# A Mamba-style mixer between two feed-forward layers: its scan in chunks of 64 positions where it went in chunks of 128

## The reference

```python
x_c, A_c, B_c, C_c = (chunk(x), chunk(Adt), chunk(Bmat), chunk(Cmat))      # CHUNK = 64
A_cum = jnp.cumsum(A_c, axis=-1)
L = jnp.exp(_segsum(A_c))                                                 # decay inside a chunk
G = jnp.einsum('bclhn,bcshn->bclsh', C_c, B_c)
Y_diag = jnp.einsum('bclsh,bcshp->bclhp', G * L, x_c)
decay_states = jnp.exp(A_cum[..., -1:] - A_cum)
states = jnp.einsum('bclhn,bclhp->bchpn', B_decay, x_c)                   # new state of each chunk
new_states = jnp.einsum('bhzj,bjhpn->bzhpn', decay_chunk, states)         # carried over the chunks
Y_off = jnp.einsum('bclhn,bchpn->bclhp', C_c, states) * state_decay_out[..., None]
y = Y_diag + Y_off + D * x
```

## Time and profile before

| | us |
|---|---|
| median of three runs | 1905.34 |
| the profiled execution | 1909.31 |
| its span, first to last instruction | 1907.5 |
| TensorE busy | 1723.2 (90%) |
| VectorE busy | 1076.9 (56%) |
| ScalarE busy | 654.0 (34%) |
| POOL busy | 436.8 (23%) |
| `decay` on TensorE, 512 matmuls | 114.4 |
| `ydiag`, 2048 records | 69.2 |
| `times_g` on VectorE, 184 | 183.8 |
| decay exponentials, 256 | 149.0 |

### The profile page before, as it was taken

How to read it: one execution, slowest core, us unless ns; L and a number is a source line. 1 busy time by engine, 2 the same in 40 slices (tenths; PEclk the granted TensorE clock), 3 DMA queues, 4 the chain that set the end, 5 groups by cost and what they waited for, 6 DMA issues and landing times.

```text
span 1907.5 us, 24623 instructions
## 1 busy us (share of the span) xinstructions
PE 1723.2 (90%) x9444; PEld 1374.8 (72%) x9444; DVE 1076.9 (56%) x1830; ACT 654.0 (34%) x1002; POOL 436.8 (23%) x310
## 2 busy tenths in 40 slices
PE   2369999976999997999998999998899998998998
PEld 0157777754888776888776788776788886777787
DVE  8953334355566755567665466766375754443233
ACT  1222222215443355433345333445334434112111
POOL 7632443010123231212232122322122323000000
PEclk7779999987999998999998899999899999999999
DMA  5373564534344443344434344444445444555564
GB/s 230 156 296 101 209 206 176 183 101 141 119 156 156 135 147 123 113 159 157 148 124 135 118 154 141 160 130 138 130 157 159 141 131 146 152 187 166 187 188 143
DMA packets 248784, 295.66 MB, mean 155 GB/s; under 512 B 11105, under 2 KB 209889, under 8 KB 238689
## 3 DMA queue, kind: packets, MB, share of 16 engines
q1 hardware_dynamic: 248672, 294.14, 46.4%
HBM read 247.97 MB, written 46.14 MB: 154 GB/s over the span
## 4 chain that ended last, share of the span: by engine, by line
PE 61%; DVE 11%; ACT 3%; issue 2%; DVEq 0%; ACTq 0%
PE bank L931 26%; PE bank L971 11%; PE bank L899 11%; PE bank L1009 3%; PE bank L1034 3%; PE bank L987 3%; DVE m_cv L1517 1%; DVE res L1503 1%; PE bank L1048 1%; PE bank L1064 1%; DVE xn L1491 1%; DVE m_L L1544 1%; DVE m_hb L1497 1%; DVE m_sta L1557 1%; PE bank L1022 1%
## 5 line engine op out<-in xcount | busy, mean ns | idle before, releaser
L931 PE MATMUL bank<-m_fxT,m_wj 128*128 128x512 f32 x2304 | 553.1, 393 | 12.7 <-DVE m_fxT L1484 4.6
L931 PEld LDWEIGHTS bank<-m_fxT,m_wj 128*128 128x128 f32 x2304 | 429.2, 189 | 105.3 <-issue 10.0
L971 PE MATMUL bank<-m_wd,m_hb 128*128 128x512 f32 x1152 | 295.2, 399 | 10.4 <-DVE res L1503 5.4
L899 PE MATMUL bank<-m_xT,m_wi 128*128 128x512 f32 x912 | 241.7, 417 | 13.8 <-DVE m_cv L1517 11.4
L971 PEld LDWEIGHTS bank<-m_wd,m_hb 128*128 128x128 f32 x1152 | 209.8, 190 | 54.6 <-issue 7.5
L1827 POOL TENSOR_TENSOR m_L<-m_L,m_GT 128x512 f32<-128x512 f32 x72 | 95.3, 1324 | 590.3 <-ACT m_L L1283 590.3
L1491 DVE SCALAR_TENSOR_TENSOR xn<-bank,m_sc,xn 128x512 f32<-128x512 f32 x96 | 72.1, 751 | 277.4 <-PE bank L931 267.4
L899 PEld LDWEIGHTS bank<-m_xT,m_wi 128*128 128x128 f32 x912 | 181.9, 203 | 56.1 <-issue 16.7
L1283 ACT ACTIVATE m_L<-bank 128x512 f32<-128x512 f32 x256 | 149.0, 596 | 208.3 <-PE bank L1009 208.0
L1503 DVE TENSOR_TENSOR res<-bank,res 128x512 f32<-128x512 f32 x192 | 129.4, 686 | 111.9 <-PE bank L971 111.4
L489 PE MATMUL bank<-fa_xT,fa_wu 128*128 128x512 f32 x768 | 185.7, 401 | 6.1 <-DMA fa_wu<-ug_split 3.5
(11 more groups left out here) (201 smaller groups left out, 1945.1 us busy)
## 6 DMA issues: line engine op xcount, KB each, us to landing
m_wj<-ug_split SPq DMA_DIRECT2D x192, 512.0 KB, 4.3
m_wd<-dn_split SPq DMA_DIRECT2D x48, 1024.0 KB, 4.8
m_wi<-in_split SPq DMA_DIRECT2D x76, 512.0 KB, 3.4
m_wo<-out_split SPq DMA_DIRECT2D x32, 512.0 KB, 4.2
ug_split<-fa_wu SPq DMA_DIRECT2D x6, 2048.0 KB, 11.6
in_split<-fa_msp SPq DMA_DIRECT2D x20, 512.0 KB, 3.0
fa_wd<-dn_split SPq DMA_DIRECT2D x8, 1024.0 KB, 6.3
fa_raw<-in_wug SPq DMA_DIRECT2D x6, 1024.0 KB, 7.0
```

The costliest lines, as they stand in the source:

```text
L899: ins = pe.matmul(PB[:], w[:, a, k, :], xT[:, b, k, :], start=(k == 0 and i == 0), stop=(k == KH - 1 and i == 2))
L931: ins = pe.matmul(to[:], w[:, a, k, :], fxT[:, b, k, :], start=(k == 0 and i == 0), stop=(k == KH - 1 and i == 2))
L971: ins = pe.matmul(F[t % 2][:], hb[:, a, j, ck(t)], wd[:, b, j, :], start=(j == 0 and n == 0), stop=(j == 1 and n == 2))
```

## The change

The chunk is 64 positions (`QL`), so there are eight chunks (`NK`) and seven chunk states (`NS`). On partitions, two heads share what 128 positions of one head had: the even heads of the block on the lower 64, the odd ones on the upper 64. A decay matrix in PSUM (one bank `A` instead of two) then holds a pair of heads for all eight chunks: four `decay` matmuls of 512 columns a block, four exponentials, three `times_g` on VectorE and one on POOL (in the last block two and two). `x_rows` turns by 16 f32 matmuls against every second group of columns of the identity, since the heads of a pair must land on different halves; before it was four transposes. `ydiag` is one call of 32 matmuls with 64 columns. `new_states` and `from_states` make seven states of two banks (`S`) instead of three of one. G and B are made for both halves in the same way.

The order changes too: all of a block's scan now stands in that block.

The core of the diff, TensorE first:

```diff
-                for i in range(2):
-                    to, by = (v.rearrange("p (c i l) -> p c i l", c=NCK, i=2)[:, :, i, :] for v in (A[n % 2][:], mvg[:]))
-                    ins = pe.matmul(to, stn[:, i, j, :], by, start=True, stop=True)
-                ins.then_inc(s_A, 1)
+                wait(pe, s_L, QUADS * (NB * q + b) + j)
+                pe.matmul(A[:], stn[:, j, :], mvg[:], start=True, stop=True).then_inc(s_A, 1)
...
-                for c in range(NCK):
-                    ins = pe.transpose(X[:, ck(c)], xc[:, b % 2, ck(c)], I)
+                for k in range(NK):
+                    for e in range(2):
+                        heads = I.rearrange("p (j e d) -> p j e d", j=QUADS, e=2)[:, :, e, :]
+                        ins = pe.matmul(X[half(e), cq(k)], xc[:, b % 2, cq(k)], heads, start=True, stop=True)
...
-                for c in range(NCK):
-                    for j in range(4):
-                        ins = pe.matmul(Y[32 * j:32 * j + 32, ck(c)], xp[:, c, 2 * j + e, :], L[:, e, j, ck(c)],
-                                        start=(e == 0 and c == 0), stop=(e == 1), skip_group_check=True)
+                for k in range(NK):
+                    for j in range(QUADS):
+                        ins = pe.matmul(Y[32 * j:32 * j + 32, cq(k)], xp[:, k, 32 * j:32 * j + 32], L[:, b % 2, j, cq(k)],
+                                        start=True, stop=True)
...
-                for c in range(3):
-                    ins = pe.matmul(SO[:, ck(c)], Bt[:, c, :], xd[:, c, :], start=True, stop=True)
+                for k in range(NS):
+                    ins = pe.matmul(S[k // 4][:, ck(k % 4)], Bt[:, k, :], xd[:, k, :], start=True, stop=True)
...
-                for c in range(1, NCK):
-                    ins = pe.matmul(SO[:, ck(c)], sta[:, c - 1, :], Cf[:, ck(c)], start=True, stop=True)
+                for k in range(1, NK):
+                    ins = pe.matmul(O[:, cq(k)], sta[:, k - 1, :], Cf[:, cq(k)], start=True, stop=True)
...
+                for k in range(NK):
+                    for e in range(2):
+                        ins = pe.matmul(X[half(e), cq(k)], Bf[:, cq(k)], Cf[:, cq(k)], start=True, stop=True)
+                ins.then_inc(s_G, 1)
+            def turn_b(q):
+                wait(pe, s_z, NB * q)
+                for k in range(NS):
+                    for e in range(2):
+                        ins = pe.matmul(S[k // 4][half(e), ck(k % 4)], Bf[:, cq(k)], I, start=True, stop=True)
+                ins.then_inc(s_B, 1)
+            def ends_out(q):
+                pe.wait_ge(s_dg, q + 1)
+                pe.wait_ge(s_gt, q + 1)
+                pe.matmul(X[:, 0:(NS - 1) * HEADS], ones[0:HEADS, :], L[0:HEADS, 1, 0, 0:(NS - 1) * HEADS],
+                          start=True, stop=True).then_inc(s_dgx, 1)
...
+                for i, (rows, n) in enumerate(((dtf, NK), (de, NS))):
+                    for k in range(n):
+                        for e in range(2):
+                            at = HEADS // 2 * (NK * i + k)
+                            ins = pe.matmul(X[half(e), at:at + HEADS // 2], rows[0:HEADS, cq(k)],
+                                            cs[0:HEADS, C_I4 + e:C_I4 + HEADS:2], start=True, stop=True)
```

On VectorE, ScalarE and POOL:

```diff
+                wait(dve, s_Y, NB * q + b)
+                for i, (to, n, done) in enumerate(((xp, NK, s_xp), (xd, NS, s_xd))):
+                    if i:
+                        wait(dve, s_S, NB * q + b)
+                    at = NK * HEADS // 2 * i
+                    by = dd[:, at:at + n * HEADS // 2].rearrange("p (k h) -> p k h", k=n)[:, :, QUADS * b:QUADS * (b + 1)]
+                    for e in range(2):
+                        ins = dve.tensor_tensor(to[half(e)].rearrange("p k (j e d) -> p k j e d", j=QUADS, e=2)[:, :, :, e, :],
+                                                X[half(e), 0:n * QL].rearrange("p (k j d) -> p k j d", k=n, j=QUADS),
+                                                by[half(e)].unsqueeze(3).to_broadcast([HALF, n, QUADS, HDIM]), ALU.mult)
+                    ins.then_inc(done, 1)
...
-                for i in range(2):
-                    at = HEADS * i + HPB * b
+                for k in range(1, NS):
+                    at = HEADS * (k - 1) + HPB * b
...
                 if more:
+                    raw(q + 1, 1, NB + 1)
                     step_ln(q + 1)
                     step_inverse(q + 1)
-                    b_silu(q + 1)
-                    raw(q + 1, 1, NB + 1)
                 beside_rows(q + 1)
-                times(q, NB - 1)
                 if more:
                     sums_high(q + 1)
                     to_end(q + 1)
+                    c_silu(q + 1)
+                    raw(q + 1, 2, 0)
...
+                    older = (q, b - 1) if b else (q - 1, NB - 1) if q else None
                     copies(q, b)
                     if b == NB - 1:
-                        times_g(q, 8 * b + 1)
-                    times_g(q, 8 * b + 3)
+                        times_g(q, b, 1)
+                    times_g(q, b, QUADS - 1)
                     if older:
                         low_part(*older)
                         add_squares(*older)
-                    times_g(q, 8 * b + 7)
+                    combine(q, b)
```

More of the change, by code:

```diff
@@ L1069, in products @@
                 pe.wait_ge(s_xcv, LCONV * q + 2)
-                wait(pe, s_z, NB * q)
-                for c in range(NCK):
-                    ins = pe.matmul(SO[:, ck(c)], Bf[:, ck(c)], Cf[:, ck(c)], start=True, stop=True)
+                wait(pe, s_ex, NB * q)
+                for k in range(NK):
+                    for e in range(2):
+                        ins = pe.matmul(X[half(e), cq(k)], Bf[:, cq(k)], Cf[:, cq(k)], start=True, stop=True)
                 ins.then_inc(s_G, 1)
             def turn_b(q):
-                wait(pe, s_ex, NB * q)
@@ L1078, in turn_b @@
-                pe.wait_ge(s_dg, q + 1)
-                for c in range(3):
-                    pe.transpose(X[:, ck(c)], Bf[:, ck(c)], I)
-                for i in range(2):
-                    at = 3 * P + HEADS * i
-                    ins = pe.matmul(X[:, at:at + HEADS], ones[0:HEADS, :], dg[:, i, :], start=True, stop=True)
-                ins.then_inc(s_B, 1)
+                wait(pe, s_z, NB * q)
+                for k in range(NS):
+                    for e in range(2):
+                        ins = pe.matmul(S[k // 4][half(e), ck(k % 4)], Bf[:, cq(k)], I, start=True, stop=True)
@@ L1092, in turn_d @@
-                for c in range(3):
-                    at = HEADS * (NCK + c)
-                    ins = pe.matmul(X[:, at:at + HEADS], de[0:HEADS, ck(c)], cs[0:HEADS, C_I4:C_I4 + HEADS], start=True, stop=True)
+                pe.wait_ge(s_bt, 3 * q + 3)
+                for i, (rows, n) in enumerate(((dtf, NK), (de, NS))):
[4 more added lines that the diff above has]
+                                            cs[0:HEADS, C_I4 + e:C_I4 + HEADS:2], start=True, stop=True)
@@ L1117, in _ @@
                     x_rows(q, b)
-                    decay(q, n)
+                    decay(q, b, 0)
                     if end and more:
@@ L1416, in _ @@
                         gate(q, b + 1)
+                    elif more:
+                        b_silu(q + 1)
                     hidden_high(at, 1)
@@ L1719, in _ @@
                     hidden(at, 0)
-                    times_g(q, n + 4)
-                    if b:
-                        carried(q, b - 1)
                     hidden_low(at, 0)
-                    if not end:
-                        times_g(q, n + 5)
+                    carried(q, b)
                     if end and more:
                         step_abs(q + 1)
-                    times_g(q, n + 6)
-                    if end and more:
                         step_one(q + 1)
+                        step_rest(q + 1)
+                        conv(q + 1, 0, NB)
+                    within(q, b)
                     hidden(at, 1)
-                    if end and more:
-                        conv(q + 1, 0, NB)
                     hidden_low(at, 1)
```

343 lines of the change are left out of this document (142 added, 201 removed).

## The result

The changed kernel takes 1946.35 us (median of 4; 1944.8 to 1948.7) against 1907.06 for the kernel before (with one more execution than the 1905.34 above): 1.0205 times as long, 95% interval 1.0183 to 1.0227. It became slower, as forecast, and the time lies in the stated range of 1930 to 2040, but outside my own of 1965 to 2022: it is 39 us more, where my 1992 would have been 85 more. The profiled execution has a span of 1943.1 us, 35.6 more than the 1907.5 of before.

The account below looks back on a forecast made before the run. TensorE, without gaps in ordinary blocks, was taken as the bound. 65 + 8.7 + 5.6 - 4.5 + 12 = +87 us on the profiled 1909.3 gave 1996, or 1992 against the median; own range 1965 to 2022, stated range 1930 to 2040.

Parts of the forecast that it names:

- 32 ordinary blocks: TensorE's decays, x's turn, diagonal products, new states and from states: +2.03 us a block, +65 us in all.
- late VectorE ahead of the first add: Scaling ahead of down's first add, behind late statistics in block 5, stalls TensorE 3.3 us: +8.7 us in all.
- block 0: One bank makes each decay wait for the previous exponential: 2.8 us over price, half already there, 1.4 times 4: +5.6 us.
- last blocks, between sequences, preparation: Block 7's idle half taken back, -4.5 us; between sequences +1.8 three times and first preparation +6.4, together +12 us.
- What bounds the kernel: TensorE has no gap in ordinary blocks, so in 32 blocks every microsecond on its queue is one of the span.
- Decays, new states, from states: TensorE's work in each block: decays -1.17 us, new states +0.92, from states +0.78.
- The floor of 110 ns: Loading a 128-wide stationary operand takes 110 ns a record on TensorE; fewer moving columns cannot bring it lower.
- the price of narrow records: TensorE: 57.8 ns a 64-wide record, x's turn +1.50 us a block; 31.6 ns at 32 wide, diagonal products unchanged.
- Rival 2: Only narrow matmuls get cheap: diagonal products halve, x's turn at 31.6 ns, 128-wide ones at the floor: 1933 us, chance 0.10.
- Between sequences: Added work +6.4 us, against waits for C's Silu going, 3.9, and clock perhaps staying up: net +1.8, three times.
- The chain of states: VectorE's 13 dependent operations, 4.2 us, hide under 5.9 us of TensorE cover while POOL is quiet: priced at nothing.

Follow-up runs that it names:

- the two orders put right: Changed kernel with scaling behind the second add of down in blocks 1 to 7 and block 0's decays spread over other matmuls: 1909.03 us, 1.0008.
- the first experiment: Changed kernel with the scaling of x moved behind the second add of the down projection in blocks 1 to 7: 1915.21 us, 1.0041.
- with two halves: Changed kernel with scaling moved and block 0's decays spread, plus from states as fourteen matmuls of 64 output partitions, halves in turn: 1886.75 us, 0.9892.
- with C's Silu late: Changed kernel with C's Silu, x's first evacuation and its conv again behind the last two copies of the beside rows: 1952.41 us, 1.0231.

## Why the prediction was right in sign and wrong in size

| term | forecast, us | spans after less before, us |
|---|---|---|
| 32 ordinary blocks | +65 | +8 |
| late VectorE ahead of the first add | +8.7 | +29 |
| block 0 | +5.6 | +16 |
| last blocks, between sequences, preparation | +8 | -19 |

The right column comes from the block lengths of both traces: 0.25 times 32; blocks 2, 5 and 6 less 0.25 each; block 0 less 0.25 and the 2.7 of scan work that now stands in it; and the last row is three stretches of -8.0 and the run-out from the last block 7's start, -8.0 too, with 2.45 put back in each (2.7 moved out, less 0.25), and +3.3 for a later start of the mixer. They sum to 34, the spans differ by 35.6. The run-out is loose: in the traces of the two other runs with chunks of 128 it is 337.6 and 338.2 us where this one has 341.4, and in those with chunks of 64 it is 333.4 to 338.5; some 3 us of the -19 may be this execution's own.

- **What bounds the kernel**: right for the ordinary blocks. TensorE has no gap in them before or after. But the larger costs of the change, +29 and +16 us, stand in waits and in the slow clock behind them.
- **Decays, new states, from states**: right, -1.12, +0.79, +0.84 for -1.17, +0.92, +0.78. The floor of 110 ns for a 128-wide record with few columns held: from states took 114.
- **The step that failed** is the price of narrow records: "I interpolate 57.8 ns for 64 wide" and "a rate that 32-wide loading sets doesn't fall with the columns". x's turn cost +0.73 us a block and not +1.50, the diagonal products -1.00 and not 0; these two are 1.77 of the 1.78 us by which the block's sum was too high, 57 us in 32 blocks. The experiments with the loops exchanged show it: 57.5 ns is right for one half at a time (that the interpolation met it is luck), 34 ns when the halves take turns, 16 ns over four strips. The interpolation mixed a rate over four strips (31.6) with one over the whole array (110). Rival 2 had both prices nearly right (31.6 ns for x's turn, half for the diagonal products); its block, +0.18, is the measured +0.25. I gave it 0.10. The Trainium skill (TensorEngine Tiling (Array Packing), "Key Properties") states that different tiles can load and multiply in parallel. The trace agrees: 34 ns a record with the halves in turn against 57.5 in one half.
- **Late VectorE**: the mechanism was right and worked out for block 5 (3.3 us stall forecast, 4.51 measured), but mis-sized twice. TensorE came 0.7 us sooner, mostly as x's turn was cheaper; the scaling took 2.7 us and not 2.3 (two operations of 0.69 and two of 0.62, the working's own prices, add to 2.6); and another 1.6 us went to the clock. And the working counted only the statistics, not the norm's end ahead of block 2. Moving the scaling took 31 us away.
- **Block 0**: the waits were priced at 2.8 us and halved, for no row. Measured, TensorE's idle time in the block went from 0.3 to 2.1 us, and the term is 4.0 a block; the rest is mostly the half clock, which the working left out. Spreading the decays gave back 13.7.
- **Between sequences**: right in part. The waits for C's Silu and behind it went, the clock stayed up for the products, and the wait before dt's turn stayed (2.67 us for 2.83). The wait of 2.66 us for ScalarE ahead of L925, in place of 1.12 and 1.26, and the slow clock behind it had no term. The added work was priced at 6.4 us, mostly by the same wrong rate and by half clock; dt's turn is 0.9 us shorter than before instead of 3.9 longer, and its mean granted clock was 0.88 where it had been 0.50. (The first preparation was not wholly at full clock before, as the working has it: dt's turn there took 3.2 us too, at 0.50.) B's turn came near its price, 1.7 us for 1.6. C's Silu is worth 4 to 6 us by experiment; the rest is not settled.
- **The chain of states**: right, no wait in any ordinary block, each step 0.32 us with POOL quiet, and the wait that came in block 0 once POOL was beside it shows the condition was real.

So the forecast was the sum of a large term eight times too big, two small ones three times too small, and a fourth of +8 that came out at -19. That the total still fell into the stated range owes something to luck, as the errors of 57 and 27 us one way met 31 the other way; and so does the sign. The working had the kernel slower because its small matmuls cost more; they cost 8 us, and with the two orders put right it is not slower (1.0008). That rival 2's 1933 would have been off by 13 the other way says the same: it had the matmuls right and the waits too small.

## What to carry to other kernels

Price small f32 matmuls by the strip of the array that they use: take the cost of one strip, and divide by the strips that take turns. That comes out somewhat low (57.5 over two is 29 where 34 was measured, 49 over four is 12 for 14.5 to 16), and a rate read off one pattern holds for that pattern. Where a 128-wide f32 matmul has only 64 columns, try splitting its outputs over strips and interleave them; at 128 columns two halves gained nothing. When a consumer's operation moves ahead of the one that a full TensorE waits for, list everything that makes that engine late in any block, and price the slow clock behind each stall as something that may or may not come.

## What the runs showed of the hardware

- f32 records with 64 moving columns and 128 rows: 114 ns at 128 output partitions, 57.5 at 64 in one half, 34 at 64 in two halves in turn, 49 at 32 in one strip, 16 at 32 over four in turn (14.5 for from states). With 128 columns: 115 to 127 at 128 output partitions, 67 at 64 in two halves in turn, 31.6 at 32 over four in turn. Splitting the seven matmuls of from states four ways took them from 1.60 to 0.81 us.
- In the blocks of the mixer with TensorE at full clock before, the granted clock fell to half behind or during every stall of 3.8 to 4.5 us, and six matmuls that take 1.4 us took 2.2. It did not fall behind the stalls of 1.23, 1.50 and 1.68 us there, nor behind the 0.77 in the kernel before. Between them it went either way: behind 1.79 us it fell in two blocks 5 of three in the first experiment and in one of three with two halves; behind 2.4 us in block 2 it fell in all three sequences of the changed kernel, and in none with C's Silu late, whose row shows six matmuls at the full rate:

```profile
849.48 1.66 PE L975 MATMUL bank<-m_wd,m_hb 128*128 128x512 f32 x6 [2.37 <-DVE res L1491]
```
